# Feed-forward of a graph layer: a curve of twelve terms, and TensorE's tile in the order curve g, output g - 1, curve turned, first product g + 2, rows g + 3

## What is computed

```python
def pwlin_gelu_basic(x, mantissa_bits_in, mantissa_bits_out):
    xq = float2fix(x, mantissa_bits_in)          # rounded to multiples of 1/256
    y = jnp.interp(xq, _PWL_X, _PWL_Y)           # GELU, 33 points on [-4, 4]
    y = jnp.where(xq > 4.0, xq, jnp.where(xq < -4.0, jnp.float32(0.0), y))
    return float2fix(y, mantissa_bits_out)

h = float2fix(jnp.einsum('bsd,df->bsf', x, w1) + b1, 8)
h = float2fix(pwlin_gelu_basic(h, 8, 8), 8)
out = float2fix(jnp.einsum('bsf,fd->bsd', h, w2) + b2, 8)
...
x = x + graph(xn) + linear(xn)                   # the sum x1 of a row
x = x + ffn(layernorm(x))
```

## Time and profile before

| | us |
|---|---|
| median of three runs | 3360.26 (3357.45 to 3362.67) |
| the profiled execution, its time | 3363.04 |
| its span | 3361.1 |
| TensorE matmuls busy | 3119.3 (93%) |
| VectorE busy | 2615.5 (78%) |
| ScalarE busy | 1227.4 (37%) |
| curve matmuls (400) | 97.0 |
| terms on ScalarE (400) | 247.9 |

### The profile page before, as it was taken

One profiled execution on the slowest core, in us unless ns is written; L12 is line 12 of the kernel. 1 busy time (PEld: TensorE's weight loads), 2 busy tenths in 40 slices (PEclk: granted clock), 3 DMA queues, 4 the chain that ended last, 5 costly groups with the idle time before them and its releaser, 6 DMA issues. The chain is left out here.

```text
span 3361.1 us, 42506 instructions
## 1 busy us (share of the span) xinstructions
PE 3119.3 (93%) x14512; PEld 2540.1 (76%) x14512; DVE 2615.5 (78%) x4560; ACT 1227.4 (37%) x1596; POOL 1009.4 (30%) x698
## 2 busy tenths in 40 slices
PE   6899999996999999898979999999999999499997
PEld 5778888865888888676667888887887888377776
DVE  5577677765777777557889999999999976577784
ACT  2011111121111111212356565566556543366665
POOL 1246776756677667650000000000000000000000
PEclk8999999998999999999999999999999999699999
DMA  7943333343444444544544453454345221433331
GB/s 252 374 93 68 60 55 67 62 121 68 90 89 90 86 88 96 125 90 140 157 129 121 126 145 105 113 135 132 103 129 154 72 62 35 129 91 87 92 92 37
DMA packets 286038, 366.20 MB, mean 109 GB/s; under 512 B 190330, under 2 KB 190430, under 8 KB 285910
## 3 DMA queue, kind: packets, MB, share of 16 engines
q1 hardware_dynamic: 95828, 282.24, 28.7%
q0 software_dynamic: 184656, 65.68, 11.2%
q10 hardware_dynamic: 5426, 16.70, 1.4%
HBM read 272.64 MB, written 90.80 MB: 108 GB/s over the span
## 5 line engine op out<-in xcount | busy, mean ns | idle before, releaser
L1447 PE MATMUL G_acc<-values,whole_plain 125*125 125x257 f32 x5000 | 1108.2, 383 | 45.8 <-DVE whole_plain L1407 30.2
L1447 PEld LDWEIGHTS G_acc<-values,whole_plain 125*125 125x125 f32 x5000 | 939.2, 189 | 204.8 <-DVE whole_plain L1407 40.9
L357 POOL DMA_INDIRECT counts<-E_twins_now,E_cells_now x400 | 867.9, 2170 | 387.1 <-issue 248.0
L1311 ACT ACTIVATE whole_plain<-whole_plain,G_asrc_slope 125x750 f32<-125x750 f32 (+1 forms) x400 | 377.8, 946 | 418.7 <-DVE whole_plain L1394 417.9
L1394 DVE SCALAR_TENSOR_TENSOR whole_plain<-whole_plain,G_asrc_most 125x750 f32<-125x750 f32 (+1 forms) x400 | 411.1, 1028 | 46.3 <-PE G_acc L1447 45.0
L1285 POOL DMA_DIRECT2D gat<-xT_plain x100 | 53.6, 536 | 959.5 <-ACT xT_plain L1327 959.5
L978 DVE SCALAR_TENSOR_TENSOR N_least<-xT_plain,asrc_all,N_least 125x750 f32<-125x750 bf16 (+1 forms) x336 | 338.9, 1013 | 0.0
L254 PE MATMUL V_v_ps<-whole,xT_space 128*125 128x512 f32 x1200 | 293.6, 402 | 29.3 <-DVE xT_space L282 20.8
L254 PE MATMUL Q_q_ps<-whole,xT_space 128*125 128x512 f32 x1200 | 288.4, 399 | 20.8 <-DVE xT_space L282 20.8
L254 PEld LDWEIGHTS V_v_ps<-whole,xT_space 128*125 128x125 f32 x1200 | 221.3, 188 | 101.3 <-DVE xT_space L282 40.1
L254 PE MATMUL K_v_ps<-K_wv,xT_space 128*125 128x512 f32 x1200 | 292.7, 400 | 0.0
(11 more groups left out here) (177 smaller groups left out, 3308.3 us busy)
## 6 DMA issues: line engine op xcount, KB each, us to landing
whole_plain<-counts SPq DMA_DIRECT2D x222, 328.1 KB
counts<-K_zeros POOLq DMA_DIRECT2D x50, 763.5 KB, 8.3
xT_whole<-xnT SPq DMA_DIRECT2D x75, 500.0 KB, 3.6
whole_plain<-counts SPq DMA_DIRECT2D x74, 382.8 KB
xnT<-xT_whole SPq DMA_DIRECT2D x25, 500.0 KB, 8.2
gat<-xT_plain POOLq DMA_DIRECT2D x100, 125.0 KB, 2.4
E_row<-edge_keys ACTq DMA_DIRECT2D x25, 488.3 KB
E_row<-edge_keys SPq DMA_DIRECT2D x25, 488.3 KB
```

The lines of the kernel that those rows point to most:

```text
L357: nc.gpsimd.indirect_dma_start(out=counts_cells, out_offset=bass.IndirectOffsetOnAxis(ap=self.cells_now[:, slot, c:c + 1], axis=0), in_=se ...
L1311: nc.scalar.activation(here, here, ACT.Exp, bias=asrc_slope[:, u % H, j:j + 1]).then_inc(exp_ready, 1)
L1447: m = nc.tensor.matmul(acc[0:T, t, 0:CW], weight[:, k % RING, t * T:(t + 1) * T], values[:, j, u % H, :], start=(j == 0), stop=(j == NT - 1))
```

## The change

It leaves out four of the sixteen terms. `CURVE` lists twelve pairs of a knot (in 256ths, no longer evenly spaced from the seventh on) and a kink; the size is held at 918/256 instead of 4. Its assertion says that the rounded curve is the same at each of the 1025 sizes.

It also moves steps. TensorE: the output product of tile g - 1 (a new function `feed`) stands right behind curve g, the turning of the curve behind that, then the first product of g + 2, then the rows of g + 3. VectorE: `hidden(g + 1)` and `split(g + 2)` at the head of the body, the layer norm (now of g + 3) ahead of `finish(g - 1)`. ScalarE: the high part of rows g + 2 and the terms of g + 1 at the head, the high part of the turned curve last. SP: the loads (now of g + 4) ahead of the store. Ahead of the loop, one `hidden`, one `split` and one `layernorm` fewer stand on VectorE before w2's low part, one `split` fewer on ScalarE before w2's high part.

```diff
@@ -56,29 +56,26 @@
 BITS = 11
 
 
-def short(x):
-    unit = 2.0 ** (math.frexp(x)[1] - BITS)
-    return round(x / unit) * unit
-
-
-def short_kinks():
-
-
-    kinks, at, slope = [], 0.0, 0.0
-    for below, above in zip(BENT, BENT[1:]):
-        kinks.append(short(4.0 * (above - at) - slope))
-        slope += kinks[-1]
-        at += 0.25 * slope
-    return kinks
-
-
-def curve(size, kinks):
-    return sum(kink * max(size - knot, 0.0) for kink, knot in zip(kinks, KNOTS))
-
-
-KINKS = [4.0 * (BENT[i + 1] - BENT[i]) - (4.0 * (BENT[i] - BENT[i - 1]) if i else 0.0) for i in range(16)]
-SHORT = short_kinks()
-assert all(round(256.0 * curve(n / 256.0, KINKS)) == round(256.0 * curve(n / 256.0, SHORT)) for n in range(1025))
+CURVE = ((0, -0.4013671875), (64, 0.185791015625), (128, 0.15234375), (192, 0.1087646484375),
+         (256, 0.060821533203125), (320, 0.02154541015625), (381, -0.00800323486328125), (450, -0.0222015380859375),
+         (513, -0.0250091552734375), (574, -0.024993896484375), (641, -0.018157958984375), (714, -0.0183258056640625))
+WHOLE_FROM = 918
+
+
+def bent(n):
+
+    i = min(n // 64, 15)
+    return 256.0 * (BENT[i] + (n - 64 * i) / 64.0 * (BENT[i + 1] - BENT[i]))
+
+
+def curve(n):
+
+
+    return sum(kink * max(min(n, WHOLE_FROM) - knot, 0) for knot, kink in CURVE)
+
+
+assert all(round(bent(n)) == round(curve(n)) and abs(curve(n) - round(curve(n))) < 0.4965 for n in range(1025))
+assert all((kink * 2.0 ** (BITS - math.frexp(kink)[1])).is_integer() for _, kink in CURVE)
 assert NT * T == N and NCH * CH == E and UNITS * CPU == NCH and UNITS == 2 * NT and sum(GROUPS) == NT
 assert E + 1 < 2 ** 16 and CNT >= N * (N + 1) and N * N + BATCH * CH <= CNT < 2 ** 24 and BATCH * CH < AGAIN
 
@@ -1462,13 +1459,14 @@
...
-    KN = len(SHORT)
+    KN = len(CURVE)
@@ -1527,17 +1525,16 @@
                 sp.dma_start(raw[:, :, :], w.rearrange("(k p) n -> p k n", p=128)).then_inc(w_loaded[i], 16)
             sp.dma_start(b1_row[:, :], a["b1"].partition_broadcast(T)).then_inc(biases_loaded, 16)
             sp.dma_start(b2_row[:, :], a["b2"].partition_broadcast(T)).then_inc(biases_loaded, 16)
-            for g in range(1, 5):
+            for g in range(1, 4):
                 sp.wait_ge(xn_ready, g)
                 load(g)
 
             def body(g, n):
+                if fixed(g, 0, NT - 5):
+                    sp.wait_ge(xn_ready, g + 4)
+                    load(g + 4)
                 if fixed(g, 1):
                     keep_out(g - 1)
-                if fixed(g, 0, NT - 6):
-                    sp.wait_ge(xn_ready, g + 5)
-                    load(g + 5)
-                if fixed(g, 1):
                     kept_out(g - 1)
             over_tiles(sp, body, **TILES)
             keep_out(NT - 1)
@@ -1569,16 +1566,15 @@
             split(0)
             split(1)
             make_terms(0, 0)
-            split(2)
             weights(1, w2, raw2)
 
             def body(g, n):
+                if fixed(g, 0, NT - 3):
+                    split(g + 2)
+                if fixed(g, 0, NT - 2):
+                    make_terms(g + 1, n + 1)
                 act.wait_ge(gelu_turned, g + 1)
                 high(nc, geluT[:, 0, :, :], gelu_tr[:, :, 0:T]).then_inc(gelu_high, 1)
-                if fixed(g, 0, NT - 2):
-                    make_terms(g + 1, n + 1)
-                if fixed(g, 0, NT - 4):
-                    split(g + 3)
             over_tiles(act, body, **TILES)
 
         @block.vector
@@ -1623,18 +1619,18 @@
                 chain.step(nc.vector.scalar_tensor_tensor(out=size, in0=here, scalar=-1.0, in1=here,
                                                           op0=ALU.mult, op1=ALU.max))
                 chain.settle()
-                nc.vector.tensor_scalar(size, size, 4.0, None, ALU.min).then_inc(size_ready, 1)
+                nc.vector.tensor_scalar(size, size, WHOLE_FROM / 256.0, None, ALU.min).then_inc(size_ready, 1)
 
             chain.step(nc.vector.memset(root[:, :], 0.0))
             for i in range(KN):
-                chain.step(nc.vector.memset(knots[:, i:i + 1], -KNOTS[i]))
+                chain.step(nc.vector.memset(knots[:, i:i + 1], -CURVE[i][0] / 256.0))
             chain.settle()
             def weights(i, w, raw):
                 for n, part in enumerate(parts_of(raw)):
                     dve.wait_ge(w_high[i], n + 1)
                     low(nc, w[:, 1, part, :], raw[:, part, :], w[:, 0, part, :]).then_inc(w_low[i], 1)
 
-            for i, kink in enumerate(SHORT):
+            for i, (_, kink) in enumerate(CURVE):
                 chain.step(nc.vector.memset(kink_row[:, i:i + 1], kink))
             chain.settle()
             nc.vector.tensor_tensor(kinks_whole, ident[0:T, 0:T].unsqueeze(1).to_broadcast([T, KN, T]),
@@ -1647,29 +1643,26 @@
             hidden(0, 0)
             split(1)
             layernorm(2, 2)
-            hidden(1, 1)
-            split(2)
-            layernorm(3, 3)
             weights(1, w2, raw2)
             ahead_of_tiles(chain)
 
             def body(g, n):
+                if fixed(g, 0, NT - 2):
+                    hidden(g + 1, n + 1)
+                if fixed(g, 0, NT - 3):
+                    split(g + 2)
                 chain.settle()
                 dve.wait_ge(bent_done, g + 1)
                 chain.step(nc.vector.scalar_tensor_tensor(out=gelu[:, :], in0=hid[:, n % 2, :], scalar=0.0, in1=bent_ps[:, :],
                                                           op0=ALU.max, op1=ALU.add))
                 chain.settle()
                 fix(gelu[:, :], gelu[:, :]).then_inc(gelu_ready, 1)
+                if fixed(g, 0, NT - 4):
+                    layernorm(g + 3, n + 3)
                 if fixed(g, 1):
                     finish(g - 1, n - 1)
                 dve.wait_ge(gelu_high, g + 1)
                 low(nc, geluT[:, 1, :, :], gelu_tr[:, :, 0:T], geluT[:, 0, :, :]).then_inc(gelu_low, 1)
-                if fixed(g, 0, NT - 5):
-                    layernorm(g + 4, n + 4)
-                if fixed(g, 0, NT - 3):
-                    hidden(g + 2, n)
-                if fixed(g, 0, NT - 4):
-                    split(g + 3)
             over_tiles(dve, body, chain=chain, steps=1 + LN_STEPS + 1 + 2, **TILES)
             finish(NT - 1, NT - 1)
 
@@ -1697,19 +1690,7 @@
             turn(2)
             pe.wait_ge(kinks_ready, 1)
 
-            def body(g, n):
-                for i in range(KN):
-                    pe.wait_ge(terms_ready, g * KN + (i + 1))
-                    last = nc.tensor.matmul(bent_ps[:, :], kinks[:, i, :], terms[:, i, :], start=(i == 0), stop=(i == KN - 1))
-                last.then_inc(bent_done, 1)
-                if fixed(g, 0, NT - 4):
-                    turn(g + 3)
-                pe.wait_ge(gelu_ready, g + 1)
-                for b in range(FB):
-                    last = nc.tensor.transpose(gelu_tr[:, b, 0:T], gelu[:, b * 128:(b + 1) * 128], ident[0:T, 0:T])
-                last.then_inc(gelu_turned, 1)
-                if fixed(g, 0, NT - 3):
-                    hidden(g + 2)
+            def feed(g):
                 pe.wait_ge(gelu_low, g + 1)
                 pe.wait_ge(fed_free, g + 1)
                 if not fixed(g, 1):
@@ -1718,7 +1699,24 @@
                     cols = slice(half * 512, (half + 1) * 512)
                     last = product(nc, fed_ps[0:T, cols], lambda s, b: geluT[:, s, b, :], lambda m, b: w2[:, m, b, cols], FB)
                 last.then_inc(fed_done, 1)
+
+            def body(g, n):
+                for i in range(KN):
+                    pe.wait_ge(terms_ready, g * KN + (i + 1))
+                    last = nc.tensor.matmul(bent_ps[:, :], kinks[:, i, :], terms[:, i, :], start=(i == 0), stop=(i == KN - 1))
+                last.then_inc(bent_done, 1)
+                if fixed(g, 1):
+                    feed(g - 1)
+                pe.wait_ge(gelu_ready, g + 1)
+                for b in range(FB):
+                    last = nc.tensor.transpose(gelu_tr[:, b, 0:T], gelu[:, b * 128:(b + 1) * 128], ident[0:T, 0:T])
+                last.then_inc(gelu_turned, 1)
+                if fixed(g, 0, NT - 3):
+                    hidden(g + 2)
+                if fixed(g, 0, NT - 4):
+                    turn(g + 3)
             over_tiles(pe, body, **TILES)
+            feed(NT - 1)
 
 
 # ---- launch: one core; inputs and outputs as the reference has them ----
```

## The result

The change takes 3302.33 us (3301.96 to 3307.5, four runs) against 3358.96 for the kernel before in the same comparison: ratio 0.9833, 95% interval 0.9821 to 0.9844. That is 56.6 us less where 49.2 were forecast, and 0.7 us outside the range. Direction and mechanism were right; several terms of the gain were sized too small. Totals vary by more than that 0.7: timed again (e11), the change was 51.0 us under the kernel before. The feed-forward stage is the firmer measure: in the traces it is 55.9 us shorter, 435.6 us against 491.5, and 435.7 in e11. The profiled executions differ by 60.9 us, of which 5.0 are an earlier start of the stage, behind code that is the same in both.

A forecast was written before the change was run, and what follows sets the result against it. The prediction took TensorE to bound the middle stretch. From the 3360.26 us median it took 49.2 (29.2 period, 2 loop ends, 12.5 start, 5.4 end), giving 3311 us, range 3303 to 3326.

The forecast's parts named there:

- The start's gain beyond the moved output: Before curve 1: 12.5 us gained, 5.6 of it moved output; a rival denied the rest, 3318 us, chance 0.06.
- The tail: From curve 22 to the end of the span: 51.5 us against 56.90, a gain of 5.4 us.
- 12 x 0.232 = 2.78 + 5.58 + 0.41 + 5.68 + 1.02 = 15.47: TensorE's steady tile: curve, output, curve turned, first product and rows turned give a 15.47 us period, 1.39 less.
- The wait of 0.46 us goes: Steady tile: TensorE's wait before turning the curve vanishes, as the output product of tile g - 1 covers VectorE's work.
- VectorE's 4 us of issue: At both loop ends: VectorE's issue stays, before the hidden stage, putting it back by about 3.3 us without harm.
- 1 us for TensorE's branch: At the loop's ends: TensorE's own branch, now behind eight short transposes, was charged 1 us in all.
- the prediction's stall for TensorE: Rival at both loop ends: TensorE stalls to fetch after its branch as VectorE does, 3319 us; chance 0.09.
- the start: Before curve 1: it starts at 2934.5 instead of 2947.01, 12.5 us earlier, of which 5.6 are paid at the end.
- faster transposes: Eight transposes taking about 0.83 us; with a warm clock in the tail, 6 to 8 us more gain.
- a warm clock in the tail: Last tiles: TensorE's clock staying up; with faster transposes, 6 to 8 us more gain.
- VectorE does not set the pace: Rival in steady tiles: VectorE's 14.41 us of work plus three waits could exceed the 15.47 us period; chance 0.10.
- The slow clock in every tile: Rival: late VectorE idles TensorE 3 us, low clock adds 5.5 us a tile, up to 3515; chance 0.03 with the like.

The follow-up runs named there:

- e11: The change unaltered, timed again beside the kernel before: 3301.63 us against 3352.58, ratio 0.9847.
- e2: The kernel before, in its old order, with the twelve new terms: 3333.48 us against 3354.83, ratio 0.9941.
- e1: The change's new order with the sixteen old terms: 3323.15 us against 3354.83 for the kernel before, ratio 0.9898.
- e6: The change with VectorE's and ScalarE's steps ahead of the loop ordered as before: 3316.53 us against 3358.13 for the kernel before, ratio 0.9868.
- e13: The change with 30 more VectorE memsets ahead of the loop, shifting its code: all TensorE periods 15.29 us, stage 437.0 us.
- e15: The kernel before with 350 more VectorE memsets ahead of its loop: 353.8 us from curve 1 to curve 22, stage 488.9 us.
- e10: The change, but VectorE keeps finish g - 1 ahead of the layer norm: 3414.9 us against 3358.13 for the kernel before, ratio 1.017.
- e3: The change with only eight of the twelve terms in the curve: period 14.37 us, stage 413.9 us.
- e4: The change with only the first four of the twelve terms in the curve: period 14.20 us, stage 409.7 us.
- e7: The change with VectorE doing the turned curve's low part first in the last two tiles: 3305.66 us against 3358.13 for the kernel before, ratio 0.9847.
- e14: The kernel before with 270 more VectorE memsets ahead of its loop: 356.1 us from curve 1 to curve 22, stage 494.0 us.

## Why the prediction was off

**Right.** TensorE bounds the middle and still does. Four terms cost 4 x 0.232 us of it (e2: 0.93; between e1 and the change 16.19 - 15.29 = 0.90). The wait before the turned curve goes. VectorE fits with 0.2 us before the curve (0.3 said) and 0.6 to 0.7 before the first product (0.7 said). The start's gain beyond the moved output is VectorE's order (e6). In a steady tile no engine waits for SP's loads, and neither TensorE nor VectorE for ScalarE. The tail was forecast at 51.5 and measured at 51.7, 50.8 in e11.

**Wrong, the step "12 x 0.232 = 2.78 + 5.58 + 0.41 + 5.68 + 1.02 = 15.47".** It took the eight transposes at their busy time, 1.02, the last 0.25 us of which the next group overlaps. By starts they cost 0.77; all other terms of the sum were taken by starts, and the text ahead of the prediction says that a pace is read so. The curve is 2.89 instead of 2.78 (with the output product behind it, as in e1, it is 0.11 us longer than with the transposes behind it; why was not tested) and the turned curve 0.35 instead of 0.41; the sum is 15.29. 21 x 0.18 = 3.8 us. The same slip sits in "The wait of 0.46 us goes". TensorE's matmul row counts the wait from the end of the transposes' busy time. The row of the weight loads in the trace of before has nearly the whole gap:

```profile
3019.51 0.41 PEld L1709 LDWEIGHTS F_gelu_tr<-ident,F_work 125*128 125x128 f32 x4 [0.70 <-DVE F_work L1590]
```

e1 shows 0.67 us a tile for the order. So the order was worth 14 us in steady tiles, not 9.7.

**Wrong, the ends of the loop.** The prediction kept VectorE's 4 us of issue and charged 1 us for TensorE's branch. Neither was there. That VectorE's issue would do no harm was right by itself (e13); that it was absent was luck: it came from where the code happened to lie (e13, e15), which nothing in the order of the instructions says. The 1 us for TensorE's branch was taken from no row, and no run shows it, not even e10. The Trainium skill's rule that the prediction weighed (Runtime: NRT & Kernel Launch, Instruction fetch mechanics: code lies in blocks, and a branch out of those held must fetch) fits VectorE in all traces, with the ends of the blocks left to choose. The same section gives TensorE's instruction memory 2048 instructions and that of most engines 512. The traces show some 960 instructions of TensorE in a turn of the loop (432 matmuls, 432 weight loads, the rest its sequencer's), so by that size its code would all be held, and the prediction's stall for TensorE "by that rule" did not follow.

**Wrong, the start.** Curve 1 came 2.1 us earlier than said. 0.6 of it is an earlier start of the first product of tile 2, the rest that product and the transposes behind it: 2927.45 - 2920.05 = 7.40 us where the prediction had 8.9. The product of the change and that of e11:

```profile
2920.05 6.79 PE L251 MATMUL F_hid_ps<-whole,xT_space 128*125 128x512 f32 x24
```

```profile
2921.62 8.25 PE L251 MATMUL F_hid_ps<-whole,xT_space 128*125 128x512 f32 x24
```

TensorE had idled 4.57 us before the turned curve just ahead of it in the one and 4.72 in the other, so the length of the wait does not say how long the clock stays low (granted 0.84 and 0.67); what does was not found. The repeats put curve 1 at 63.6 to 64.0 us, so about 1 of the 2.1 us is chance. In e11 the 8.9 us are there, and the 1.0 lies in the earlier turning of the curve alone.

Together 3.8 + 1.0 + 2.1 - 0.2 = 6.7 us, and 49.2 + 6.7 = 55.9, which is what the stage shows. All three lean the same way. The range's lower end had 6 to 8 us for "faster transposes" and "a warm clock in the tail"; the period took half of that, the clock in the tail was not warm (8.43 us for the last product), and the start and the branch were not in it.

**The rivals.** VectorE does not set the pace at twelve terms. With eight it had no wait left (e3); by its floor of 14.20 us and TensorE's 14.37 it would bind from seven down, an estimate. TensorE's branch does not stall. The slow clock in every tile is real as a mechanism, but smaller than priced: the prediction had 5.5 us a tile for it, behind a wait of 3 us, and in e10 a wait of 3.36 us cost 1.5 us more, as only the curve ran slow. It took an order of VectorE that the change does not have.

## What to carry to other kernels

Take a group of matmuls by the starts of it and of the next group, and a gap on TensorE by the row of its weight loads (0.70 us where the matmul row had 0.46, and 0.67 were gained); busy time runs on into the next group. When TensorE's order moves, move the order of the engine that feeds it too and lay both out from one start: the whole change gained 51 to 57 us or cost 57, by whether one step of VectorE stood before or behind another (e10). A gap on TensorE of 2.5 to 3.5 us cost more than itself in these runs, as the clock fell behind it (by 1.3 us or more in e2, e4 and e10, and by up to 2.6 in the tail); look for the instruction that another engine could do first (e7).

## What was not expected of the hardware

The place of a loop's code decides whether VectorE pays 2.4 to 4.5 us at each of the two branches back: 30 instructions more ahead of the loop brought it back, and 350 more took it away in the kernel before, which made that kernel's middle 3.4 us shorter. How much of it TensorE feels depends on the cover: 3.3 us in two turns before, 2.2 in e14, 8.4 in e2, nothing in e13.
